# Query and key channels in position-first, head-second order in a windowed attention block

## The reference

```python
h = layer_norm(x, ln1_g, ln1_b)
hp = jnp.pad(h, ((0, 0), (0, pad_h), (0, pad_w), (0, 0)))   # 16 x 16 -> 28 x 28
win = ...                                                   # 4 windows of 14 x 14 per image
q, k, v = split(win @ qkv_w + qkv_b)                        # 12 heads of 16
attn = einsum('bnd,bmd->bnm', q * KD ** -0.5, k)
bias_h = einsum('bhwc,hkc->bhwk', rq, Rh)                   # decomposed relative position
bias_w = einsum('bhwc,wkc->bhwk', rq, Rw)
attn = softmax(attn + bias_h[..., :, None] + bias_w[..., None, :])
o = (attn @ v) @ proj_w + proj_b                            # windows put back, padding cut off
x2 = x + o
m = gelu(layer_norm(x2, ln2_g, ln2_b) @ mlp_w1 + mlp_b1) @ mlp_w2 + mlp_b2
out = x2 + m
```

## Time and profile before

| | us |
|---|---|
| median of 3 runs | 367.52 (366.74 to 368.96) |
| profiled execution | 364.25 |
| its span, first to last instruction | 362.4 |
| TensorE busy in it | 301.5 (83%) |
| VectorE, ScalarE, GpSimd busy | 165.5, 130.2, 82.4 |

### The profile page before, as it was taken

How to read it: one execution, slowest core, us unless ns; L and a number is a source line. 1 busy time by engine, 2 the same in 40 slices (tenths; PEclk the granted TensorE clock), 3 DMA queues, 4 the chain that set the end, 5 groups by cost and what they waited for, 6 DMA issues and landing times.

```text
span 362.4 us, 5230 instructions
## 1 busy us (share of the span) xinstructions
PE 301.5 (83%) x1980; PEld 208.2 (57%) x1980; DVE 165.5 (46%) x435; ACT 130.2 (36%) x245; POOL 82.4 (23%) x122
## 2 busy tenths in 40 slices
PE   0899889999793957849569759759998999999996
PEld 0433575566562744637346636535776655959596
DVE  4934571255772635536356457633639911111011
ACT  1244742234462525425245435534400165040400
POOL 3184800020011202202123213119104740000000
PEclk9999989999699789887898898985865599999999
DMA  5750086892046859558667567493100000000001
GB/s 149 190 139 0 2 91 106 149 123 61 2 54 109 89 97 130 65 99 95 96 132 117 99 106 120 136 220 86 27 12 0 1 0 2 22 24 22 22 31 57
DMA packets 19937, 27.92 MB, mean 77 GB/s; under 512 B 6196, under 2 KB 16916, under 8 KB 18088
## 3 DMA queue, kind: packets, MB, share of 16 engines
q1 hardware_dynamic: 17368, 24.93, 40.7%
q0 software_dynamic: 2016, 2.46, 2.8%
q10 hardware_dynamic: 528, 0.20, 0.3%
HBM read 5.79 MB, written 1.57 MB: 20 GB/s over the span
## 4 chain that ended last, share of the span: by engine, by line
PE 50%; DMA 22%; SPq 14%; DVE 10%; issue 2%; ACT 2%; ACTq 0%; DVEq 0%
DMA qop<-bias 18%; PE ps L1212 9%; PE ps L1227 9%; PE ps L916 7%; PE ps L971 5%; SPq L293 5%; PE ps L951 5%; SPq L307 3%; PE ps L1005 3%; SPq L294 3%; PE ps L1044 2%; DMA qop<-shift 2%; PE ps L1070 2%; PE ps L1054 1%; SPq L290 1%
## 5 line engine op out<-in xcount | busy, mean ns | idle before, releaser
L739 DVE TENSOR_REDUCE nmax<-ps 98x2 f32<-98x392 f32 x96 | 53.4, 566 | 72.1 <-PE ps L1005 71.3
L1005 PE MATMUL ps<-kop,qop 126*98 126x196 f32 x192 | 43.7, 322 | 31.3 <-DMA qop<-bias 29.3
L1005 PEld LDWEIGHTS ps<-kop,qop 126*98 126x98 f32 x192 | 30.1, 204 | 43.4 <-DMA qop<-bias 33.1
L548 ACT ACTIVATE pm<-ps 98x784 f32<-98x784 f32 x48 | 39.6, 827 | 25.0 <-PE ps L1044 24.8
L1044 PE MATMUL ps<-qop,kop 128*98 128x196 f32 x192 | 32.5, 303 | 4.5 <-DMA qop<-shift 3.9
L1227 PE MATMUL ps<-w2t,gl 128*128 128x192 f32 x192 | 32.0, 328 | 0.0
L1227 PEld LDWEIGHTS ps<-w2t,gl 128*128 128x128 f32 x192 | 31.1, 190 | 0.7 <-issue 0.7
L1044 PEld LDWEIGHTS ps<-qop,kop 128*98 128x98 f32 x192 | 27.8, 214 | 6.4 <-DMA qop<-shift 4.0
L420 POOL DMA_DIRECT2D den<-osb x11 | 7.1, 648 | 98.6 <-ACT osb L565 98.6
L744 DVE TENSOR_REDUCE nmax<-ps 120x1 f32<-120x316 f32 x48 | 23.1, 485 | 12.1 <-PE ps L1011 10.1
L616 ACT ACTIVATE gl<-ps,b 128x512 f32<-128x512 f32 x24 | 16.4, 689 | 33.9 <-PE ps L1212 33.8
(11 more groups left out here) (127 smaller groups left out, 461.2 us busy)
## 6 DMA issues: line engine op xcount, KB each, us to landing
qop<-bias SPq DMA_DIRECT2D x8, 448.0 KB
kop<-hl SPq DMA_DIRECT2D x12, 280.5 KB
qop<-hl SPq DMA_DIRECT2D x12, 256.0 KB
kop<-hl SPq DMA_DIRECT2D x12, 140.2 KB
bias<-in_x SPq DMA_DIRECT2D x4, 384.0 KB, 3.8
qop<-hl SPq DMA_DIRECT2D x12, 128.0 KB
xres<-in_x SPq DMA_DIRECT2D x2, 768.0 KB, 9.5
out<-xn SPq DMA_DIRECT2D x8, 192.0 KB, 2.0
```

Of the source, the lines that this page charges most:

```text
L548: a.activation(pm[0:HALF, gi], ps[0:HALF, b0:b0 + 2, 0:2 * WIN], ACT.Exp).then_inc(s["exp_done"], 1)
L739: v_.tensor_reduce(nmax[0:HALF, h % 2, 2 * n:2 * n + 2], ps[0:HALF, bank, 0:2 * WIN].rearrange("p (t k) -> p t k", t=2), AX.X, ALU.max, ne ...
L1005: o = mm(ps[0:HALF, bank, WIN * t:WIN * (t + 1)], q[0:R_MAX, WIN * n + HALF * t:WIN * n + HALF * (t + 1)], kk[0:R_MAX, WIN * n:WIN * (n + ...
```

## The change

Channels of q and k are laid out position first and head second: channel d of head h is partition 8d + h in `xf0`, `xf1`, `hl0`, `hl1`; in the third tile it is 8d + (h - 8) for q and 8d + 4 + (h - 8) for k. A head's 16 rows are thus every eighth partition. The weights are loaded as they are, in two transfers, and GpSimd copies the q and k columns in the new order into `wqp` (in space that `bias8` takes later), in eight copies. The vectors are loaded a second time in the new order (`vecp`). The rows of `bias8` change places by half (`bias_row`), and the tables are made in three instructions.

```diff
         def place(h):
             if h < A8:
-                return (0, KD * h), (1, KD * h)
-            return (2, KD * (h - A8)), (2, 64 + KD * (h - A8))
+                return (0, h), (1, h)
+            return (2, h - A8), (2, HEADS - A8 + h - A8)
+
+        def bias_row(h):
+            return (h + A8 // 2) % A8
...
             sp.dma_start(vec[:], vectors).then_inc(s["vec_in"], 16)
+            sp.dma_start(vecp[:], vectors.rearrange("(h d) c -> d h c", h=A8)).then_inc(s["vec_in"], 16)
             load_x(1)
             for wt, r0, r1 in ((wq0, 0, P), (wq1, P, C)):
-                for d0, s0, n in ((0, 0, P), (P, C, P), (2 * P, P, C - P), (2 * P + C - P, C + P, 2 * C - P)):
-                    sp.dma_start(wt[:, d0:d0 + n], qkv_w[r0:r1, s0:s0 + n]).then_inc(s["w_in"], 16)
+                sp.dma_start(wt[:], qkv_w[r0:r1]).then_inc(s["w_in"], 16)
...
             for j in range(A8):
-                sp.dma_start(relc[KD * j:KD * (j + 1)], rel).then_inc(s["rel_in"], 16)
+                sp.dma_start(relc[j:P:A8], rel).then_inc(s["rel_in"], 16)
...
-                src = hl[tq][rq:rq + KD, :, 0:T]
+                src = hl[tq][rq:P:A8, :, 0:T]
                 sp.dma_start(q[0:2 * KD], src).then_inc(sl, 16)
                 sp.dma_start(q[2 * KD:R_BIAS], src[:, 0]).then_inc(sl, 16)
-                src = hl[tk][rk:rk + KD]
+                src = hl[tk][rk:P:A8]
                 sp.dma_start(k[0:2 * KD], src[:, 0:1].to_broadcast([KD, 2, KCOLS])).then_inc(sl, 16)
                 sp.dma_start(k[2 * KD:R_BIAS], src[:, 1]).then_inc(sl, 16)
...
-                    sp.dma_start(q[R_BIAS:R_MASK], bias8[h:h + A8 * (WS - 1) + 1:A8]).then_inc(sl, 16)
+                    sp.dma_start(q[R_BIAS:R_MASK], bias8[bias_row(h):A8 * WS:A8]).then_inc(sl, 16)
...
+            pool.wait_ge(s["w_in"], 2 * 16)
+            for wt, w in ((wq0, wqp[0]), (wq1, wqp[1])):
+                src = wt[:, 0:2 * C].rearrange("p (m h d) -> p m h d", m=2, h=HEADS)
+                for m in range(2):
+                    g.tensor_copy(w[:, P * m:P * (m + 1)].rearrange("p (d h) -> p h d", h=A8), src[:, m, 0:A8]
+                                  ).then_inc(s["wqp_ready"], 1)
+                dst = w[:, 2 * P:3 * P].rearrange("p (d m h) -> p m h d", m=2, h=HEADS - A8)
+                for m in range(2):
+                    g.tensor_copy(dst[:, m], src[:, m, A8:HEADS]).then_inc(s["wqp_ready"], 1)
             normalise(2)
...
-                pe.wait_ge(s["w_in"], 8 * 16)
+                pe.wait_ge(s["wqp_ready"], 8)
```

More of the change, by code:

```diff
@@ L101, in window_attention_block @@
         ps = ctx.enter_context(nc.psum_tensor("ps", [P, 8, 512], F32))
-        end, (ident, vec, vshift, bs, stats, mv, var, std, rstd, nmr, nmax, parts, parts_rest, shift, shift_rest, den,
+        end, (ident, vec, vecp, vshift, bs, stats, mv, var, std, rstd, nmr, nmax, parts, parts_rest, shift, shift_rest, den,
               v_main, v_rest, v_pad, kst, qop0, qop1, kop0, kop1) = room(
-            base, ("ident", [P, P]), ("vec", [P, 32]), ("vshift", [P, C]), ("bs", [P, 3]), ("stats", [P, NT, 6]),
+            base, ("ident", [P, P]), ("vec", [P, 32]), ("vecp", [P, 32]), ("vshift", [P, C]), ("bs", [P, 3]), ("stats", [P, NT, 6]),
             ("mv", [P, NT, 2]), ("var", [P, NT]), ("std", [P, NT]), ("rstd", [P, NT]), ("nmr", [P, NT]),
@@ L139, in window_attention_block @@
         xt = bias8[:, 0].rearrange("p l t -> p (l t)")[:, 0:NT * C].rearrange("p (t c) -> p t c", t=NT)
+        wqp = [bias8[:, 0].rearrange("p l t -> p (l t)")[0:r, NT * C + 3 * P * k:NT * C + 3 * P * (k + 1)]
+               for k, r in enumerate((P, C - P))]
         htw = (bias4[:, 0], bias4[:, 1])
@@ L165, in window_attention_block @@
             "rd0_in", "rd1_in", "xb2_ready", "pads_ready", "c0_in", "c1_in", "c2_in", "reld_ready", "htw_ready",
-            "xn_early", "v_zero", "p_zero", "low_in", "low_in1", "low_in2",
+            "xn_early", "v_zero", "p_zero", "wqp_ready", "low_in", "low_in1", "low_in2",
         )}
@@ L377, in relative_tables @@
                 pool.wait_ge(s["rel_in"], 16 * A8)
[L378 to L381, removed]
+                n = A8 // 2
+                for d, h0 in ((reld8[:, :, :, n:A8], 0), (reld8[:, :, :, 0:n], n), (reld4[:], 0)):
+                    g.tensor_tensor(d.rearrange("p a r j -> p (a r) j"),
+                                    relc[:].rearrange("p a r -> p (a r)").unsqueeze(2).to_broadcast([P, 2 * (2 * WS - 1), n]),
+                                    vecp[:, 24 + h0:24 + h0 + n].unsqueeze(1).to_broadcast([P, 2 * (2 * WS - 1), n]),
                                     ALU.mult).then_inc(s["reld_ready"], 1)
@@ L474, in unit @@
                 a.activation(xf[m][:, c * CHUNK:(c + 1) * CHUNK], ps[:, 4 + u % 4, :], ACT.Identity,
-                             scale=vec[:, SCL + m:SCL + m + 1], bias=bs[:, m:m + 1]).then_inc(s["xf_ready"], 1)
-            act.wait_ge(s["vec_in"], 2 * 16)
+                             scale=vecp[:, SCL + m:SCL + m + 1], bias=bs[:, m:m + 1]).then_inc(s["xf_ready"], 1)
+            act.wait_ge(s["vec_in"], 3 * 16)
             std_of(0)
@@ L650, in _ @@
             v_.memset(v_rest[:, :, :, KD:VD], 1.0)
-            dve.wait_ge(s["vec_in"], 2 * 16)
-            v_.tensor_tensor(bs[:], vec[:, BQKV:BQKV + 3], vec[:, SCL:SCL + 3], ALU.mult).then_inc(s["bs_ready"], 1)
+            dve.wait_ge(s["vec_in"], 3 * 16)
+            v_.tensor_tensor(bs[:], vecp[:, BQKV:BQKV + 3], vecp[:, SCL:SCL + 3], ALU.mult).then_inc(s["bs_ready"], 1)
             def early_stats(c):
@@ L891, in _ @@
             mm = nc.tensor.matmul
-            pe.wait_ge(s["vec_in"], 2 * 16)
+            pe.wait_ge(s["vec_in"], 3 * 16)
             def transposes(c, src, done, banks, evac, n):
@@ L914, in project @@
                         pe.wait_ge(s["xf_ready"], u - 3)
-                    for k, (wt, ht) in enumerate(((wq0, ht0), (wq1, ht1))):
+                    for k, (wt, ht) in enumerate(((wqp[0], ht0), (wqp[1], ht1))):
                         o = mm(ps[:, 4 + u % 4, :], wt[:, P * m:P * (m + 1)], ht[:, cols], start=(k == 0), stop=(k == 1))
@@ L935, in relative_bias @@
                 if v == 0:
-                    pe.wait_ge(s["reld_ready"], 2)
+                    pe.wait_ge(s["reld_ready"], 3)
                 if v < 4:
```

## The result

| | before | after |
|---|---|---|
| median, us | 367.56 (366.74 to 368.96, 4 runs) | 339.42 (338.49 to 341.83, 4 runs) |
| profiled execution, us | 364.25 | 338.49 |
| its span, us | 362.4 | 336.6 |

The ratio is 0.9241, with a 95% interval of 0.9185 to 0.9297. Lines have moved: L290 to L294 are L297 to L301 in the changed kernel, L302 and L307 are L309 and L314, L916 is L933, L1005 is L1022, L1054 is L1071.

The account below looks back on a forecast made before the run. The bound was taken as a load loop closed through TensorE's program order, slowed by reading adjacent rows. Loads -22.2, `vecp` +0.43 and VectorE beside GpSimd +0.2 gave -21.5 us: 346.0 us, range 335 to 357.

Parts of the forecast that it names:

- rival B: `hl` loads: only the reading side has the limit, gain 3.83 us a load, 337.1 us in all; chance 0.25.
- the prediction's own signs: Load loop: first periods of 12.3 us would show the forecast right; 200 GB/s throughout and a period under 11, rival B.
- A: `hl` loads, the forecast: spaced reads help two thirds of the bytes, 346.0 us; chance 0.50.
- part 1: `hl` loads of heads 3 to 11: spaced source rows save 12.8 us plus 9.4 us, -22.2 us.
- the term for rows 32 to 47: `hl` loads: writes into 16 adjacent rows as slow as such reads, 2.62 us for 268.2 KB, gain 2.55 a load.
- TensorE's floor: Heads 8 to 11: TensorE's own work, 9.3 to 10.9 us a head by clock, sets the period, taken as 10.7.
- +0.43 for `vecp`: Front: one more load issue ahead of `load_x(1)` delays VectorE's start and all that follows by 0.43 us.
- +0.2 for VectorE beside GpSimd: Front: GpSimd's copies lengthen roughly 1 us of VectorE's work by 25%, booked as 0.2 us.
- the cover: Front: GpSimd's eight copies end at 10.3 us, before the first projection, costing nothing with 3.9 us to spare.
- D: `hl` loads: destination rows set the 105 GB/s, so spacing the source does nothing, 368.1 us; chance 0.07.
- E: Nine `hl` loads: rows spaced by eight read more slowly than adjacent ones, 390 us; chance 0.05.
- C: Loads gain half as much, through other queues' packets or TensorE more at 1.2 GHz: about -11 us, 356.5; chance 0.13.

Follow-up runs that it names:

- the order experiments: TensorE runs weights(h, 5) ahead of score piece 0 of head h+2: 353.08 us in the kernel before, 329.86 us and again 331.44 us in the changed kernel.
- the second profile of the changed kernel: Profile from running the changed kernel once more, unedited, on the same chip: 336.61 us.
- the repetition of the reordered change: Changed kernel with weights(h, 5) ahead of score piece 0 of head h+2 on TensorE, second measurement with six runs: 331.44 us.
- the reordered kernel before: Kernel before with weights(h, 5) ahead of score piece 0 of head h+2 on TensorE: 353.08 us.

## Why the prediction was right, and where it was off

**The bound and the cause** were read rightly. The loop of load, L1005, L1054 and the next load was the bound; the order experiments show that it was closed through TensorE's program (15 us from the order alone, though 22 had been expected of it), and the run with spaced sources alone shows that the source rows set the rate. But the time is in the range because the range was drawn to hold rival B; by the prediction's own signs (about 200 GB/s throughout a load, a first period under 11) it is B that came, and A, the forecast, missed by 6.6 us.

**The size of part 1 was off.** The step is the term for rows 32 to 47: "If writing into 16 adjacent rows is as slow as reading from 16 adjacent rows ... I take 2.55, since a port that serves reads slowly will probably serve writes no faster." The gain per load was 13.4 - 9.8 = 3.6 us (13.64 - 10.02 in the mean of heads 3 to 7), close to rival B's 3.83. No run has all writes wide, so what the narrow third costs in the changed kernel isn't known; the 0.2 us between the two are a hint at most. Rival B's reason was not quite the truth either: narrow writes do have a limit, but a milder and later one (132 to 139 GB/s after a start at 181 to 197). That both sides of a transfer count alike, as the prediction had it, isn't borne out either: reads of 16 adjacent rows ran at 103 to 116. With one row set in each of read and write and no row that separates them, I should have kept the two ends and leaned on neither; the bound from 2.55 to 3.83 did hold the value.

**What is late next.** Heads 3 to 7 got 10.86 us where A gave 12.26 and B 10.98. Of the 3.95 us saved a head, 3.62 are the load; the other 0.33 are the two L1022 and four L1071 behind it, which took 1.17 us in the mean before (1.42 in three periods of five, 0.85 in the other two, by the start of the next issue) and 0.84 in every period after. I had booked nothing for that, and B's period is met partly by this luck.

For heads 8 to 11 I booked TensorE's floor at 10.7; it was 11.17, a gain of 1.88 a head where 2.35 had been forecast. The floor wasn't what set it. Here the failed step is that no new wait would take the loads' place: TensorE stood 4.0 us for `shift_rest` in these four heads, more than the 2.0 us for bias rows, and one of the four periods runs through that transfer on the chain; in the other three the load itself (10.0 to 11.0 us) still closes the loop. So part 1 came to 19.8 + 7.5 = 27.3 us for 12.8 + 9.4: too little in the first five heads, a little too much in the last four. Why the loads of the last heads, with their shorter bias load and a second queue beside it, gained only about 2 us each was not tested.

The clock was worth more than I gave it: TensorE's busy time in the loop went from 92 to 82 us (85 in the second profile of the changed kernel), though most of that only widens the slack, since a load still sets the pace in most periods.

**The front.** I booked +0.43 for `vecp` and +0.2 for VectorE beside GpSimd. The timeline of the changed kernel:

```profile
4.91 0.16 DVE L669 TENSOR_TENSOR bs<-vecp 128x3 f32<-128x3 f32 x1 [0.26 <-DMA vecp<-in_vectors]
8.77 1.52 DVE L707 TENSOR_SCALAR bias<-bias,rstd,nmr 128x192 f32<-128x192 f32 x4
8.97 0.83 POOL L399 COPY bias<-wq 128x128 f32<-128x128 f32 x2 [5.09 <-DMA wq<-in_qkv_w]
9.65 0.53 POOL L403 COPY bias<-wq 128x64 f32<-128x64 f32 x2
10.04 0.81 POOL L399 COPY bias<-wq 64x128 f32<-64x128 f32 x2
10.60 1.37 DVE L707 TENSOR_SCALAR bias<-bias,rstd,nmr 128x192 f32<-128x192 f32 x4
10.70 0.56 POOL L403 COPY bias<-wq 64x64 f32<-64x64 f32 x2
13.88 6.78 PE L933 MATMUL ps<-ht,bias 128*128 128x512 f32 x12
```

`vecp` cost nothing on balance: VectorE waits for it (it is issued behind `vec`, and the chain passes through its landing), but that landing came at 4.89 us, where `vec` had landed at 5.12 before, and VectorE began at 4.91, sooner than before (5.14). The eight copies took 2.3 us (2.6 forecast), from 8.97, later than the 7.7 I had, to 11.3, and the first projection at 13.88 didn't wait for them: the cover holds with 2.6 us to spare. VectorE's two groups of four normalisations took 1.52 and 1.37 us; in the same view of the kernel before they are

```profile
9.00 1.25 DVE L690 TENSOR_SCALAR bias<-bias,rstd,nmr 128x192 f32<-128x192 f32 x4
...
10.57 1.25 DVE L690 TENSOR_SCALAR bias<-bias,rstd,nmr 128x192 f32<-128x192 f32 x4
```

so +0.4 us in all, where I had +0.2. In this profile each instruction is only lengthened. Two other runs with the same front show more. In the repetition of the reordered change one normalisation takes 1.00 us, where one takes 0.38 in the kernel before; it starts just ahead of the first copy and ends after the second:

```profile
9.30 1.00 DVE L707 TENSOR_SCALAR bias<-bias,rstd,nmr 128x192 f32<-128x192 f32 x1
9.36 0.67 POOL L399 COPY bias<-wq 128x128 f32<-128x128 f32 x2 [5.48 <-DMA wq<-in_qkv_w]
```

There the group of four takes 2.16 us in place of 1.25, and TensorE's first transposes start at 11.31, not at 10.44 as in the first profile. The run with q spaced and k adjacent has the same picture (one of 1.01 us, the group 2.18). So the cost of the copies depends on where they fall: 0.4 us in this profile, 0.9 in those two. That answers to the Trainium skill's rule of the shared port pair (SBUF — State Buffer, Who interferes with whom) in kind: one instruction can stand for the length of two copies. A block for all 2.3 us of the copies is not what any of these rows show. The 0.8 us by which the loop began later in this profile can't be charged to the change: in the second profile of the same kernel it began at 103.53 (103.60 before), and with the old front and every second row at 104.37. Between such executions the same front shifts by 0.8 us; the first twelve L933 here ran 6.57 us on the chain where L916 had run 6.13 (with the old front and every second row 6.43, in the second profile of the changed kernel 6.13), for a reason that was not looked for.

**Rivals.** D and E are excluded by the rates. C's mechanism, other queues' packets, is real (the shifts, 4.0 us of waits in heads 8 to 11) but far from the 11 us that C needed, and the clock rose where C had it fall.

## What to carry to other kernels

When transfers between on-chip buffers are all busy and yet slow, look at how their rows lie: reading 16 adjacent partitions halved the rate against every second or every eighth, and writing 16 adjacent ones lowered it more mildly (132 to 139 GB/s, after the first 2 us). Find the loop that a buffer's reuse closes and see which instruction in program order stands inside it; here moving four small matmuls ahead of a waiting one gave 15 us in the kernel before and some 7 to 10 more on top of the change. A fix of one wait should be followed to the next: where TensorE's waits for loads came to 29.3, 8.3 and 1.0 us, the mean granted clock of the loop was 0.86, 0.97 and 1.00, which moves the floor. The order isn't strict (0.91 with 6.9 us of waits, in the run with spaced sources alone).

## What the runs showed that I had not expected

Writes into 16 adjacent rows started at 197 GB/s and fell to 132 only after 2 us. A transfer of 3.8 KB from ScalarE's queue took 6 to 7 us when issued among SyncE's loads (6.87 in the changed kernel, issued at 170.93 where the loads of head 9 began at 169.70), which makes the order of small and large transfers worth planning. And in the reordered kernel before, the first periods alternated between about 11 and 14 us: with three buffers, a load that is longer than one head's work costs every second head.
